# Moving the causal mask into the spare rows of the shift product, and loading the image on 96 partitions so that no spreading is needed

## What is computed

```python
pooled = x.reshape(64, 12, 14, 16, 14, 16).sum(axis=(3, 5))
h = concat([einsum('bcij,ce->bije', pooled, channel_weights), txt])   # (64, 228, 192)
q, k, v = rope(split((norm_scale * layernorm(h) + norm_bias) @ W_attn + b_attn))
att = softmax([sink, where(causal, q @ k.T / 4, -inf)])[..., 1:]
h = h + ((att @ v) @ W_proj + b_proj) * rezero
h = h + moe(layernorm(h))          # top-2 of 8 experts, capacity 1.25 * 2 * N / 8
```

## Time and profile before

| | us |
|---|---|
| median of 3 runs | 2946.89 |
| the profiled execution, its own time | 2948.84 |
| its span, from first to last instruction | 2947.0 |
| TensorE busy in the span | 2785.7 (95%) |
| VectorE busy | 2049.3 (70%) |
| GpSimd busy | 2023.1 (69%) |
| ScalarE busy | 1693.0 (57%) |
| first image load issued, last image load issued | 27.9, 1631.9 |

### The profile page before, as it was taken

One profiled execution on the slowest core, in us unless ns is written; L12 is line 12 of the kernel. 1 busy time (PEld: TensorE's weight loads), 2 busy tenths in 40 slices (PEclk: granted clock), 3 DMA queues, 4 the chain that ended last, 5 costly groups with the idle time before them and its releaser, 6 DMA issues. The chain is left out here.

```text
span 2947.0 us, 65980 instructions
## 1 busy us (share of the span) xinstructions
PE 2785.7 (95%) x21712; PEld 2512.3 (85%) x21712; DVE 2049.3 (70%) x5657; ACT 1693.0 (57%) x4074; POOL 2023.1 (69%) x2070
## 2 busy tenths in 40 slices
PE   2899999999999999999999976999999999999998
PEld 0788888888888888888888865999999989998997
DVE  3477777777777777777777745777676767676766
ACT  0365666666666666656666644656565656555655
POOL 2478888888888888888888833666555656565665
PEclk9899999999999999999999987999999999999999
DMA  6444555543444444334444113333333333323242
GB/s 177 145 163 162 172 177 182 160 117 106 109 116 121 121 121 117 110 104 115 121 121 121 54 43 68 50 60 56 63 50 61 56 61 54 66 45 66 44 70 43
DMA packets 206006, 292.47 MB, mean 99 GB/s; under 512 B 95670, under 2 KB 167675, under 8 KB 205874
## 3 DMA queue, kind: packets, MB, share of 16 engines
q1 hardware_dynamic: 82994, 243.82, 28.3%
q0 software_dynamic: 122880, 47.00, 11.3%
HBM read 201.73 MB, written 93.90 MB: 100 GB/s over the span
## 5 line engine op out<-in xcount | busy, mean ns | idle before, releaser
L1493 POOL DMA_INDIRECT out<-arena,who x320 | 596.0, 1862 | 292.1 <-DVE who L1372 179.7
L686 POOL TENSOR_TENSOR arena<-arena 112x896 f32<-112x896 f32 x192 | 403.0, 2100 | 44.0 <-DMA arena<-in_x 44.0
L571 DVE TENSOR_REDUCE top<-bank 114x2 f32<-114x456 f32 (+1 forms) x576 | 352.7, 622 | 87.3 <-PE bank L930 71.1
L1466 PE MATMUL bank<-w_dn,hid 128*114 128x192 f32 x3840 | 401.9, 264 | 0.0
L1466 PEld LDWEIGHTS bank<-w_dn,hid 128*114 128x114 f32 x3840 | 390.3, 180 | 0.0
L1439 ACT ACTIVATE arena<-bank 128x456 f32<-128x456 f32 x320 | 176.3, 551 | 341.8 <-PE bank L1430 331.8
L1284 POOL DMA_INDIRECT moe_rows<-row,slot x256 | 294.5, 1150 | 77.3 <-issue 73.7
L548 ACT ACTIVATE pieces<-bank 64x456 fp32r<-64x456 f32 x384 | 209.4, 545 | 147.1 <-PE bank L906 144.8
L1443 DVE TENSOR_TENSOR arena<-bank,arena 128x456 f32<-128x456 f32 x320 | 201.5, 630 | 94.9 <-ACT arena L1439 82.4
L726 POOL TENSOR_TENSOR qk<-rot_c,qk 114x384 fp32r<-114x384 f32 x256 | 253.9, 1014 | 18.3 <-ACT qk L747 18.3
L1426 PE MATMUL bank<-pieces 128*128 128x456 f32 x640 | 240.2, 375 | 22.5 <-DVE arena L1443 15.5
(11 more groups left out here) (171 smaller groups left out, 7211.4 us busy)
## 6 DMA issues: line engine op xcount, KB each, us to landing
arena<-in_x SPq DMA_DIRECT2D x64, 2352.0 KB, 11.9
arena<-moe_rows SPq DMA_DIRECT2D x82, 363.4 KB
moe_rows<-filler SPq DMA_DIRECT2D x20, 1453.5 KB
out<-h SPq DMA_DIRECT2D x64, 171.0 KB
out<-arena,who POOLq DMA_INDIRECT x320, 5.0
arena<-in_w_t SPq DMA_DIRECT2D x9, 512.0 KB, 6.8
arena<-in_w_t SPq DMA_DIRECT2D x18, 256.0 KB, 7.7
moe_rows<-row,slot POOLq DMA_INDIRECT x256, 7.1
```

What stands on the lines that cost most here:

```text
L571: nc.vector.tensor_reduce(dst, src, AX.X, ALU.max).then_inc(maxed[k], 1)
L686: nc.gpsimd.tensor_tensor(xin[at.par][:, g, 0:mid], xin[at.par][:, g, 0:mid], xin[at.par][:, g, mid:XF], ALU.add).then_inc(x_folded, 1)
L1466: ins = nc.tensor.matmul(dst, hid2[:, j, h_part, at], w_dn2[e_par][:, j, w_part, :], start=(j == 0 and s % 2 == 0 and part == 0), stop=(j ...
L1493: nc.gpsimd.indirect_dma_start(out=out[:, :], out_offset=bass.IndirectOffsetOnAxis(ap=who[par][:, s:s + 1], axis=0), in_=ys[par][:, s, :], ...
```

## The change

**Mask.** The twelve heads are split into two groups of six. The maxima, remainders and ones of a group then take 14 rows (`TOP`), and the other 114 rows of `shift_t` hold the causal mask, written once in the setup. `sel` has an identity in those rows, so the products that subtract the maximum also add the mask. The products L956 and L959 go. `shift_t` gets two groups and three column blocks (first half of the queries with mask, second half without, second half with mask). `turn_shift` makes four transposes of 14 columns in place of two of 128; `round_shift` rounds 456 columns in place of 228, on 14 partitions; `split_shift` is two instructions, of 456 and of 228 elements, in place of one of 228.

**Image.** A partition now holds one channel and one of eight row pairs, for all 14 patch rows: 96 partitions with 14 x 448 elements. The load is eight DMAs (one for each row pair), each of 12 partitions with 14 pieces of 1792 bytes. Fold and pool work in three bands of 5, 5 and 4 patch rows (1120, 1120 and 896 elements). `pooled` has one column for each patch, so it is TensorE's operand itself: `spread_patches` and `patch` go, and `sum_channels` makes two products in place of six.

**Order.** On VectorE, pool_image(p, 2) moves from before the max of C7 to between place_k(a, 1) and split_shift(m). On GpSimd, fold_image(p, 2) moves from before add_rotation(a, 1) to after low_parts, where spread_patches was.

```diff
-        sel[h, h] = -1
-        sel[HEADS + h, h] = -1
+        sel[h % PAIRS, h] = -1
+        sel[PAIRS + h % PAIRS, h] = -1
+        sel[TOP + q, h, q] = 1
+    low[TOP:, 0] = low[TOP:, 2] = later.T
...
-        x_img = x.rearrange("b (g c) (q r) w -> b (c q) g (r w)", g=NG, r=HALF)
+        x_img = x.rearrange("b c (i r s) w -> b r c i (s w)", r=HALF, s=2)
...
-            sp.dma_start(xin[at.par][:, :, :], x_img[at.b, :, :, :]).then_inc(x_loaded[at.par], 16)
+            for r in range(HALF):
+                sp.dma_start(xin[at.par][CH * r:CH * (r + 1), :, :], x_img[at.b, r, :, :, :]).then_inc(x_loaded[at.par], 16)
...
+            lo, hi = BANDS[g]
             ins = nc.vector.tensor_reduce(
-                pooled[at.par][:, g, :],
-                xin[at.par][:, g, 0:XF // 2].rearrange("p (r j c) -> p j r c", r=HALF // 2, c=PATCH), AX.XY, ALU.add)
+                pooled[at.par][:, SIDE * lo:SIDE * hi],
+                xin[at.par][:, lo:hi, 0:IMG].rearrange("p i (j c) -> p i j c", c=PATCH), AX.X, ALU.add)
...
-            nc.vector.scalar_tensor_tensor(out=shift_t[:, :], in0=shift_hi[:, :].bitcast(fp32), scalar=split[:, 2:3],
-                                           in1=bank[7][:, 0:T], op0=ALU.mult, op1=ALU.add).then_inc(shift_ready, 1)
+            turned = bank[7][0:TOP, 0:4 * TT].rearrange("p (g t n) -> p g t n", g=2, t=2)
+            for to, of in ((slice(0, 2), slice(0, 2)), (slice(2, 3), slice(1, 2))):
+                ins = nc.vector.scalar_tensor_tensor(out=shift_t[0:TOP, :, to, :], in0=shift_hi[:, :, of, :].bitcast(fp32),
+                                                     scalar=split[0:TOP, 2:3], in1=turned[:, :, of, :], op0=ALU.mult, op1=ALU.add)
+            ins.then_inc(shift_ready, 1)
...
-            nc.gpsimd.tensor_tensor(xin[at.par][:, g, 0:mid], xin[at.par][:, g, 0:mid], xin[at.par][:, g, mid:XF],
+            lo, hi = BANDS[g]
+            nc.gpsimd.tensor_tensor(xin[at.par][:, lo:hi, 0:IMG], xin[at.par][:, lo:hi, 0:IMG], xin[at.par][:, lo:hi, IMG:XF],
                                     ALU.add).then_inc(x_folded, 1)
-
-        def spread_patches(pool, at):
...
-                for g in range(NG):
-                    ins = nc.tensor.matmul(bank[6][0:hi - lo, D * t:D * (t + 1)], spread[:, g, lo:hi], chan[:, g, :],
-                                           start=(g == 0), stop=(g == NG - 1))
+                ins = nc.tensor.matmul(bank[6][0:hi - lo, D * t:D * (t + 1)], pooled[at.par][:, lo:hi], chan[:, :],
+                                       start=True, stop=True)
...
-                ins = nc.tensor.matmul(dst[0:TT, 0:2 * T].rearrange("p (a n) -> p a n", a=2)[:, :, 0:TT], ident_r[0:TT, 0:TT],
-                                       mask_k[:, 0:2, :], start=False, stop=True)
...
-                nc.tensor.matmul(dst[0:TT, 0:4 * TT], ident_r[0:TT, 0:TT], mask_k[:, :, :], start=True, stop=False)
...
             maxima("6")
-            if p:
-                pool_image(dve, p, 2)
             maxima("7 8")
...
                 place_k(dve, a, 1)
+            if p:
+                pool_image(dve, p, 2)
             if m:
                 split_shift(dve, m)
```

More of the change, by code:

```diff
@@ L21 @@
 HALF = PATCH // 2
[L22 to L25, removed]
+XP = CH * HALF
+XF = 2 * IMG
+BANDS = ((0, 5), (5, 10), (10, SIDE))
+NG = len(BANDS)
 D = 192
@@ L28 @@
 PAIRS = HEADS // 2
+TOP = 2 * PAIRS + 2
 TXT = 32
@@ L67, in constants @@
     split[:, 1] = np.where(term >= 2, -1, 0)
-    split[HEADS:2 * HEADS, 2] = -1
-    split[2 * HEADS + 1, 3] = -1
+    split[PAIRS:2 * PAIRS, 2] = -1
+    split[2 * PAIRS + 1, 3] = -1
     small = np.zeros((128, 2 * E + 2), f)
@@ L84, in constants @@
         "mask_q0": np.ascontiguousarray(np.repeat(later[:, None], 4, 1)),
-        "mask_k": np.ascontiguousarray(np.repeat(later.T[:, None], 4, 1)),
+        "low": low,
         "sel": sel,
@@ L89, in constants @@
         "before": (q[:, None] < q[None, :]).astype(f),
-        "patch": ((rows[:, None] // 2) % SIDE == np.arange(SIDE)[None]).astype(f),
         "filler": filler,
     }
-CONST_NAMES = ["cos", "sin", "ident", "mask_q0", "mask_k", "sel", "split", "small",
-               "before", "patch", "filler"]
+CONST_NAMES = ["cos", "sin", "ident", "mask_q0", "low", "sel", "split", "small",
+               "before", "filler"]
 class Batch:
@@ L179, in build @@
         gate = sb("gate", [C, 2, E])
[L183 to L186, removed]
+        arena = sb("arena", [128, 2 * SIDE * XF])
+        xin = [arena[0:XP, SIDE * XF * i:SIDE * XF * (i + 1)].rearrange("p (i f) -> p i f", i=SIDE) for i in range(2)]
+        pooled = [sb(f"pooled{i}", [XP, SIDE * SIDE]) for i in range(2)]
         h = [sb(f"h{i}", [TT, 2, D]) for i in range(2)]
@@ L209, in build @@
         top = sb("top", [TT, 2, HEADS])
-        shift = sb("shift", [TT, 2, 128])
-        shift_hi = sb("shift_hi", [128, T], fp32r)
-        shift_t = sb("shift_t", [128, T], fp32r)
+        shift = sb("shift", [TT, 2, 2, TOP])
+        shift_hi = sb("shift_hi", [TOP, 2, 2, TT], fp32r)
+        shift_t = sb("shift_t", [128, 2, 3, TT], fp32r)
         prob = sb("prob", [128, HEADS * T])
         staging, start = {}, 0
-        for name, rows, width in (("mask_q0", TT, 4 * TT), ("mask_k", TT, 4 * TT), ("sel", 128, HEADS * (TT + 1)),
+        for name, rows, width in (("mask_q0", TT, 4 * TT), ("low", 128, 3 * TT), ("sel", 128, HEADS * (TT + 1)),
                                   ("before", TT, TT), ("sink_col", 128, HEADS)):
@@ L257, in view @@
             taken += a * b
-            assert taken <= 2 * NG * XF
+            assert taken <= 2 * SIDE * XF
             return arena[0:parts, taken - a * b:taken].rearrange("p (a b) -> p a b", a=a)
@@ L371, in setup_sync @@
                     sp.dma_start(dst, src).then_inc(loaded, 16)
-            for g in range(NG):
-                sp.dma_start(chan[:, g, :], chan_w[GRP * g:GRP * (g + 1), :].unsqueeze(1)
-                             .to_broadcast([GRP, SIDE * 2, D])).then_inc(loaded, 16)
-            for name in ("mask_q0", "mask_k", "sel", "before"):
+            sp.dma_start(chan[:, :], chan_w.unsqueeze(0).to_broadcast([HALF, CH, D])).then_inc(loaded, 16)
+            for name in ("mask_q0", "low", "sel", "before"):
                 src = const[name]
@@ L442, in setup_vector @@
             dve.wait_ge(step0, n)
-            for tile in (xn[:, :, :, C:C1], yn[:, :, :, C:C1], shift[:, :, 2 * HEADS:2 * HEADS + 2],
+            for tile in (xn[:, :, :, C:C1], yn[:, :, :, C:C1], shift[:, :, :, 2 * PAIRS:TOP],
                          val[0][:, :, :, HD:HD + 1], val[1][:, :, :, HD:HD + 1]):
@@ L937, in turn_shift @@
             wait(pe, routed, at.b - 1)
-            for t in range(2):
-                ins = nc.tensor.transpose(bank[7][:, TT * t:TT * (t + 1)], shift[:, t, :], ident[0:TT, 0:TT])
+            for g in range(2):
+                for t in range(2):
+                    ins = nc.tensor.transpose(bank[7][0:TOP, TT * (2 * g + t):TT * (2 * g + t + 1)], shift[:, t, g, :],
+                                              ident[0:TT, 0:TT])
             ins.then_inc(shift_turned, 1)
@@ L1254, in one @@
                 if p:
-                    spread_patches(pool, p)
+                    fold_image(pool, p, 2)
                 if gone:
```

63 lines of the change are left out of this document (27 added, 36 removed).

## The result

The kernel after takes 3337.93 us (median of 4 runs, 3316.04 to 3341.59) where the kernel before takes 2947.18: 1.130 times as long (interval 1.1267 to 1.1331). The forecast was 2924 and the range ended at 2958. The loss lies in the first pass.

| | before | after |
|---|---|---|
| first 21 steps (filler rows written too), each | 26.1 | 39.3 |
| the other 41 steps, each | 25.75 | 28.3 |

The account below looks back on a forecast made before the run. TensorE's order of work was taken to set the step; 0.7 us saved less 0.25 lost gave -27 us over some 60 steps, plus 3 for setup: 2923 to 2924, forecast 2905 to 2940, wider range 2870 to 2958.

Parts of the forecast that it names:

- TensorE's savings: Mask products save 1.2 us a step, `sum_channels` 1.33, two added transposes cost 0.2: 2.3 us a step, 9%.
- What is added elsewhere: VectorE: larger bands 0.23 each, split 0.6 more; ScalarE: rounding 0.18 more; GpSimd: 0.5 us lighter in sum.
- The chains: Dependencies through other engines, C5 to T0 and T0 to `turn_yn`, absorb much of TensorE's saving, leaving 0.45 us a step.
- the sum: Whole step: 0.7 us saved, 0.25 lost, so 0.45 shorter; setup and first image cost 3 us once.
- the DMA rival: First 20 steps: DMA engines become the bound, costing at most 14 us (2938); sign turns at 160 ns a packet; chance 0.05.
- a rule of the Trainium skill: Image load: a DMA uses the largest engine count up to 16 dividing both sides' slowest dimension, twelve for 12 partitions.
- The second chain: From T0 to `turn_yn`: VectorE's tail grows, TensorE stalls 1.5 us, and `turn_yn` starts 0.25 us later, counted from C5.
- GpSimd by its folds: GpSimd becomes the bound if folds run long; at 0.7 us more each, the kernel takes 2976; chance 0.11.
- More play: Chains have more slack, so most of TensorE's saving arrives: 2862 if one gives 1 us a step, 2804 for all; chance 0.16.

Follow-up runs that it names:

- e7: Kernel before with the mask part alone, image load and order of work unchanged: 2912.23 us, ratio 0.985.
- e5: Kernel after with only one of the eight image DMAs issued and `make_shift` reading one operand in SBUF: 2946.08 us, ratio 0.997 to the kernel before.
- e9: Kernel after with each of the eight image DMAs writing 12 partitions that lie 8 apart: 3134.63 us, ratio 1.059 to the kernel before.
- e1: Kernel before with each image load cut into four DMAs of 112 rows, pieces of 1792 bytes: 2957.6 us, ratio 0.9999.
- e4: Kernel after with only one of the eight image DMAs issued, `make_shift` unchanged: 3092.85 us, ratio 1.045 to the kernel before.
- e3: Kernel after with `make_shift` as two reduces, one operand in SBUF each: 3439.22 us, ratio 1.162 to the kernel before.
- e10: Kernel after with image DMAs writing 12 partitions 8 apart and `make_shift` reading one operand in SBUF: 3178.65 us, ratio 1.078 to the kernel before.
- e12: Kernel before with each image load cut into eight DMAs of 14 rows 8 apart: 3209.65 us, ratio 1.086.
- e14: Kernel after, partitions 8 apart, one-operand `make_shift`, each of eight image DMAs bringing one patch row of fourteen: 3191.89 us, ratio 1.082 to the kernel before.
- e13: Kernel before with each image load cut into twelve DMAs of all 112 rows, pieces of 1792 bytes: 2978.06 us, ratio 1.008.
- e2: Kernel before with each image load cut into ten DMAs of at most 12 neighbouring rows, pieces of 7168 bytes: 3842.75 us, ratio 1.300.
- e11: Kernel before with each image load cut into eight DMAs of 14 neighbouring rows: 3653.88 us, ratio 1.237.

## Why the prediction was wrong

*TensorE's savings.* Right as far as the runs tell them apart. The mask alone gave 1.5% (e7), 0.8 us a late step of the 1.2 read from start to start; by the chains it was to be 0.4 to 0.5, so for this part they had some more play than was read. `turn_shift` lasts 0.55 by its record where it had 0.39, so 0.16 for the added pair (0.2 reckoned); `sum_channels` has 0.86 for its four records.

*What is added elsewhere.* The sizes held: a fold of 1120 takes 2.58 where 2.6 was predicted and one of 96x896 takes 2.09, so pieces with gaps cost nothing; the two splits 0.96 from start to start (0.97); the rounding 0.54 (0.55).

*The chains.* Their sum, 25.3 a step, holds only for the steps at full clock. e5, nearly without the three things below, has 25.1 to 25.2 in 39 of 62 steps and the 1.2 us wait of `turn_yn` for normalize (1.5 predicted); the small wait for GpSimd in front of T0 is there as well (0.24 in each step, 0.3 predicted). But the sum put that stall at its own length, and nothing on what it does to the clock. In the steps where the granted clock falls to 0.94 or 0.88, a step is 1.2 to 3.2 us longer; on average the late steps are 25.95, and what is left of the predicted 23 us of gain is 8 (2946.08 against 2953.99). In e7, where TensorE doesn't wait there, the clock stays at 1.00. So the clock behind that stall was put at nothing without a reason. By e5's ratio, 0.9973, the kernel would take 2939 of 2947: within the forecast's 2905 to 2940, but with most of the gain spent.

*The step that failed first: the DMA rival's price.* It was weighed by the packet, 73 to 106 ns, on sixteen or twelve engines, which made 6 to 12 us of a load and at most 14 us in sum. The packet measured 221 ns and a load 24.8 us, and the first 21 steps alone lost 277 us. The text even named 160 ns as the point at which the sign turns, and put 0.05 on it. What no term held was where the twelve rows lie: moving them 8 apart took 203 us off (e9). Which engines a DMA uses had been weighed by a rule of the Trainium skill, and that stays open (the load held 0.80 x 16 = 12.8 engines' time, e1's on 112 rows as much). The rule on ports, cited under e9, spoke against the change and was not applied.

*The second step that failed: fold_image(p, 2) was moved beside `make_shift`.* The second chain counted what each moved instruction lasts and what it waits for, and not what runs beside it on the other engine. `make_shift`, not touched in length, went from 588 to 1964 ns, TensorE waited 1.6 in front of `turn_shift`, and its clock fell behind that. The earlier trace rows name the fold's operands (`arena` twice), and the kernel shows those of `make_shift` (`top`, `sink_tok`). A smaller share of it may be in the trace before, where `make_shift` lasted 207 at the least and 588 in the median; GpSimd is in `spread_patches` about then, 0.51 for each of three (not tested). The Trainium skill ("SBUF — State Buffer", Who interferes with whom) says that a VectorE instruction with two inputs in SBUF contends with a GpSimd instruction that reads SBUF, and calls such contention "an exclusive lock"; 2.02 beside 2.08 agrees. In e4 against e5 it is worth 147 us.

*The third step that failed: eight issues in place of one.* The sum put them at +3 us once, at 0.32 each. They take 7.6 us in each step, and beside them releases between other engines come up to 3 to 4 us late. In the kernel after, this hardly shows (no `remote` wait from 900 to 1300 us): the lock and the slow load already make everything late there. It takes their place as each is removed, which is why e3 and e10 came out slower than what they mended.

*GpSimd by its folds*, the rival with 0.11, did not happen. *More play*, with 0.16, did not in the kernel after; of it the runs show only the 0.3 to 0.4 us of e7.

The parts don't add up one by one. From the kernel after: rows apart -203; then the lock +44; then the issues moved -185; together 2993.91, within 1.6% of before. What stays open is how issues delay a semaphore between other engines, and what makes it worse: it is strong in e3, e10, e12 and e14, milder in e13 (12 issues of 0.53) and almost absent in e2 and e11 (few rows, but 0.49 an issue). No run here tells the share of the sequencer from that of the queue. Why the late steps of e2 and e11, 41.0 and 37.5, are so much longer than those of the kernel after, whose DMAs also write 12 neighbouring rows, is open as well. Nor was the image on 96 partitions tried in a single DMA.

## What to carry to other kernels

Price a split DMA by where its rows lie in SBUF and by how long its issues take in each step (0.49 to 1.2 us each here), not only by bytes and packets: the same bytes went at 97 or 164 GB/s by the partitions' spacing, and the issues alone cost 185 us in one place of the step and hardly any in another. Give a stall of TensorE a price of its own in the clock, too. When an instruction is moved, list what now runs beside it and how many operands each reads from SBUF. And when a mend makes a kernel slower, look for the third cause that the first two had covered; here the part worth having was the mask alone, 2912.23 us (e7).

## What was not expected of the hardware

- A release between two engines (TensorE to ScalarE) arrived about 3 us late beside SyncE's eight issues of DMAs of 12 rows, whether they carried 2.4 MB or a fourteenth of it (e10: 3.19; e14: 3.1).
- An issue on SyncE takes from 0.49 to 1.2 us late in the pass, and the number of rows doesn't set it: 0.49 with 12 or 14 neighbouring rows of 7168-byte pieces (e2: 4.9 for 10; e11: 3.9 for 8), 0.53 with 112 rows (e1: 2.2 for 4; e13: 6.4 for 12), 0.95 where the 12 rows are 12 channels (after and e9: 7.6 for 8), 1.2 with 14 rows 8 apart (e12: 9.8 for 8).
- Pieces of 1792 bytes over 112 rows are as fast as pieces of 7168: 105 ns each, no difference in time (e1).
- A 207 ns instruction was stretched to 2.02 us by one on another engine; a wait of 1.6 us then stood in front of TensorE, and eleven microseconds at a granted clock of 0.56.
